# Gate rows stacked as two rounded parts, expert results turned half by half, two output biases moved from GpSimd to TensorE

## Time and profile before

| | us |
|---|---|
| median of 3 timed runs (lowest to highest) | 660.68 (659.87 to 660.93) |
| the profiled execution | 657.71 |
| its span, first to last instruction | 655.92 |
| TensorE busy in the span | 611.8 (93%) |
| VectorE busy | 484.3 (74%) |
| ScalarE busy | 358.9 (55%) |
| GpSimd busy | 201.1 (31%) |
| mean granted clock of TensorE, share of full speed | 0.949 |

### The profile page before, as it was taken

How to read it: one execution, slowest core, us unless ns; L and a number is a source line. 1 busy time by engine, 2 the same in 40 slices (tenths; PEclk the granted TensorE clock), 3 DMA queues, 4 the chain that set the end, 5 groups by cost and what they waited for, 6 DMA issues and landing times.

```text
span 655.9 us, 11543 instructions
## 1 busy us (share of the span) xinstructions
PE 611.8 (93%) x3408; PEld 441.0 (67%) x3408; DVE 484.3 (74%) x1247; ACT 358.9 (55%) x634; POOL 201.1 (31%) x454
## 2 busy tenths in 40 slices
PE   8999999898999879988999899999997999989996
PEld 5784788556676547855666548888775777744785
DVE  6666799968676468988653539999869888565796
ACT  6333455425666444535565228888734565623785
POOL 4211646540002113521120106666530000211462
PEclk9987999978999989999999769999997999997899
DMA  9225999010000017810002046777310000003571
GB/s 290 70 87 166 216 205 205 14 48 3 11 20 3 2 33 180 200 33 2 6 4 74 0 153 207 238 243 242 112 32 2 3 27 3 4 0 109 176 245 58
DMA packets 32526, 61.10 MB, mean 93 GB/s; under 512 B 6434, under 2 KB 21314, under 8 KB 32476
## 3 DMA queue, kind: packets, MB, share of 16 engines
q1 hardware_dynamic: 31900, 59.46, 31.6%
q10 hardware_dynamic: 576, 1.02, 0.5%
HBM read 55.64 MB, written 4.29 MB: 91 GB/s over the span
## 4 chain that ended last, share of the span: by engine, by line
PE 78%; DVE 11%; ACT 5%; issue 3%; DMA 1%; POOL 1%; DVEq 0%; SPq 0%; ACTq 0%
PE PS L744 12%; PE PS L745 12%; PE PS L746 12%; PE PS L1004 5%; PE PS L912 4%; PE PS L987 4%; PE PS L588 3%; PE PS L775 3%; PE PS L984 2%; PE PS L1021 2%; ACT pT L1307 2%; PE PS L960 1%; PE PS L809 1%; DVE qst L1660 1%; PE PS L941 1%
## 5 line engine op out<-in xcount | busy, mean ns | idle before, releaser
L479 POOL TENSOR_TENSOR wpair<-ring,ones_col 128x128 fp32r<-128x128 f32 (+1 forms) x150 | 66.7, 444 | 171.4 <-PE PS L746 104.8
L1307 ACT ACTIVATE pT<-PS 128x512 f32<-128x512 f32 x160 | 92.7, 595 | 45.8 <-PE PS L987 37.4
L1601 DVE TENSOR_TENSOR PS<-PS,qst 128x512 f32<-128x512 f32 x134 | 93.2, 696 | 20.7 <-ACT PS L1200 18.3
L1607 DVE TENSOR_TENSOR hid_lo<-PS,hid_hi 128x512 fp32r<-128x512 f32 x150 | 102.4, 683 | 1.7 <-ACT hid_hi L1206 1.3
L1206 ACT ACTIVATE hid_hi<-PS 128x512 fp32r<-128x512 f32 x150 | 89.2, 594 | 19.7 <-DVE PS L1601 19.4
L744 PE MATMUL PS<-xhi,wpair 128*128 128x512 f32 x204 | 85.5, 419 | 0.5 <-DVE PS L1589 0.4
L745 PE MATMUL PS<-xlo,wpair 128*128 128x512 f32 x204 | 83.4, 409 | 0.0
L746 PE MATMUL PS<-xhi,wpair 128*128 128x512 f32 x204 | 83.1, 407 | 0.0
L481 POOL TENSOR_TENSOR wpair<-ring,wpair 128x128 fp32r<-128x128 f32 (+1 forms) x150 | 76.8, 512 | 11.8
L1200 ACT ACTIVATE PS<-PS,ring 128x512 f32<-128x512 f32 x88 | 58.3, 662 | 30.3 <-PE PS L746 29.4
L987 PE MATMUL PS<-qst,kz 128*128 128x256 f32 x256 | 64.6, 337 | 2.9 <-ACT pT L1307 2.9
(11 more groups left out here) (236 smaller groups left out, 1101.3 us busy)
## 6 DMA issues: line engine op xcount, KB each, us to landing
qst<-gates SPq DMA_DIRECT2D x44, 512.0 KB, 4.9
qst<-gates SPq DMA_DIRECT2D x46, 256.0 KB, 5.7
ring<-in_mlp SPq DMA_DIRECT2D x48, 128.5 KB, 3.1
ring<-in_glu SPq DMA_DIRECT2D x27, 192.0 KB, 5.7
kz<-keys SPq DMA_DIRECT2D x36, 96.0 KB
keys<-qst SPq DMA_DIRECT2D x6, 512.0 KB, 3.6
qst<-kfull SPq DMA_DIRECT2D x96, 4.0 KB
wq<-in_wq SPq DMA_DIRECT2D x3, 256.0 KB, 3.5
```

Source lines behind the costliest of these rows:

```text
L479: pool.tensor_tensor(wpair[:, pair, 0, c], w, ones, ALU.mult).then_inc(M["wstep"], 1)
L1307: act.activation(pT[:, w % 8, :], PS[:, 2 + w % 2, :], ACT.Exp, scale=sc).then_inc(A["p"], 1)
L1601: dve.tensor_tensor(o, src, row, ALU.mult).then_inc(M["hid"], 1)
L1607: dve.tensor_tensor(hid_lo[:, kept, :], PS[:, gate_bank(glu, kept), :], hid_hi[:, kept, :].bitcast(f32), ALU.subtract).then_inc(M["lo"], 1)
```

## The change

- *Gate rows as a stack.* The turned table is rounded by ScalarE (both halves) into partitions 0 to 31 of `row_pair`, VectorE subtracts and writes the rest into partitions 32 to 63, both `f32r`. A spread is one rounded product over 64 rows with a matrix that picks the row twice. ScalarE then makes both plain copies `gate_rows`, which only the DRAM store needs. The rows go to banks 0 and 1 in layers 0 and 1. `row_pair` lies where the split query weights were, so the keys of layer 2 move to `hid_hi`/`hid_lo`.
- *Start of the result banks.* In layers 2 and 3 the zero products are gone; the biases are split in setup (four small VectorE operations, and one for the picking matrix) and added by two rounded products per half. In layer 2 the unit-matrix products go ahead of the fillers.
- *Order at the route.* The table is turned before the up-projections of units 2 and 3, not behind them; fillers there are 6 and 6 in layers 2 and 3 (8 and 4 before).
- *Turn by halves.* `turn_back(L, 0)` stands before the last down-projection, `turn_back(L, 1)` behind it; ScalarE copies both halves. Fillers behind it: 8 in layers 0 and 1, none in layer 2 (16 each before).
- *Masked counts of layer 3.* Two before the turning of the normalised tile, one behind it, one behind the first query projections; fillers there 2, not 6.
- *Output biases.* `output_bias` and the transfers of `bo` are gone. The bias lies with the other bias rows, and `project_outputs` starts its bank with one product of ones and bias, before it waits for its operand.
- *SyncE.* In layer 1 the keys of layer 2 are saved ahead of the gates. The output is stored in two halves.

```diff
+        row_pair = wqpair[0:2 * EP, :, :]
+        rows_hi, rows_lo = row_pair[0:EP, :, :], row_pair[EP:2 * EP, :, :]
...
@@ SyncE, load_ring
+                if L == 1:
+                    save_keys(2)
                 save_gates()
                 first_gates()
                 if L == 1:
-                    save_keys(2)
                     stack_keys(2, range(1))
...
@@ TensorE
+            def turn_back(L, hf):
+
+                pe.wait_ge(y_out, NHALF * L + hf + 1)
+                for k in range(4):
+                    i = 4 * hf + k
+                    mm = pe.transpose(PS[:, 2 + hf, k * P:(k + 1) * P], yT[:, i * P:(i + 1) * P], ident)
+                mm.then_inc(y_turned, 1)
...
                     if first:
                         pe.wait_ge(M["hid"], kept % 2 + 1)
+                        pe.wait_ge(rt["lo"], NHALF * L + hf + 1)
...
-                        w = consts[0:EP, C_ID3 + entry:C_ID3 + entry + 1].broadcast_to([EP, P])
-                    pe.matmul(PS[:, gate_bank(glu, kept), :], w, gate_rows[:, hf, :], start=True, stop=True).then_inc(M["spread"], 1)
+                        if first and unit >= 2:
+                            pe.wait_ge(rows_out, NHALF * L + hf + 1)
+                        w = pick_one[:, entry:entry + 1].broadcast_to([2 * EP, P])
+                    pe.matmul(PS[:, gate_bank(glu, kept), :], w, row_pair[:, hf, :], start=True, stop=True).then_inc(M["spread"], 1)
...
-                keep_busy(0, (0, 2, 8, 4)[L])
+                if L == 2:
+                    pe.wait_ge(set_dve, 3)
+                    for hf in range(NHALF):
+                        c = slice(hf * HALF, (hf + 1) * HALF)
+                        pe.matmul(PS[:, hf, :], eye[:, :], xhi[:, c], start=True, stop=False, skip_group_check=True)
+                        pe.matmul(PS[:, hf, :], eye[:, :], xlo[:, c], start=False, stop=False, skip_group_check=True)
+                keep_busy(5 if L == 2 else 4 if L == 3 else 0, (0, 2, 6, 6)[L])
+                turn_rows(L)
                 if not glu:
                     for u in (2, 3):
                         up(u, 1, 1, u % 2)
-                turn_rows(L)
-                pe.wait_ge(rows_out, NHALF * (L + 1))
...
+                    if glu:
+                        pe.wait_ge(rows_out, NHALF * L + hf + 1)
+                        mm = pe.matmul(PS[:, hf, :], zerob[:, 0:P], zerob[:, :], start=True, stop=False, skip_group_check=True)
+                    else:
+                        for part in range(2):
+                            mm = pe.matmul(PS[:, hf, :], b2pair[L][:, part, :], row_pair[:, hf, :], start=(L == 3 and part == 0),
+                                           stop=False, skip_group_check=True)
...
-                if L < 3:
-                    keep_busy(4, 16)
+                turn_back(L, 1)
+                if L < 2:
+                    keep_busy(4, 8)
...
@@ project_outputs
-                    pe.wait_ge(A["fin_e"], pre["fin_e"] + hf + 1)
                     if hf == 1:
                         pe.wait_ge(A["p"], pre["p"] + adds_of[L]["p"])
+                    if L != 2:
+                        r = 2 * WIDE + 2 * P + (L // 2) * P
+                        pe.matmul(PS[:, 1 + hf, :], ones2[:, 0:P], brow[:, r:r + P].unsqueeze(1).broadcast_to([P, 4, P]),
+                                  start=True, stop=False, skip_group_check=True)
+                    pe.wait_ge(A["fin_e"], pre["fin_e"] + hf + 1)
...
@@ ScalarE, experts
-                act.wait_ge(rt["tr"], NHALF * (L + 1))
-                act.activation(gate_rows[:, 1, :], PS[0:EP, 7, :], ACT.Copy).then_inc(rows_out, 1)
+                for hf in range(NHALF):
+                    act.wait_ge(rt["tr"], NHALF * L + hf + 1)
+                    act.activation(rows_hi[:, hf, :], PS[0:EP, row_bank(L, hf), :], ACT.Copy).then_inc(rt["hi"], 1)
+                for hf in range(NHALF):
+                    act.wait_ge(rt["lo"], NHALF * L + hf + 1)
+                    act.activation(gate_rows[:, hf, :], PS[0:EP, row_bank(L, hf), :], ACT.Copy).then_inc(rows_out, 1)
```

More of the change, by code:

```diff
@@ L56 @@
 WIDE = HGRP * P
-BROWS = 2 * WIDE + 2 * P
+BROWS = 2 * WIDE + 4 * P
 C_ALL = C_BAND + TB * S
@@ L1205, in first_part @@
                         act.wait_ge(M["y"], u + 1 + UP_AHEAD - KEPT)
+                    elif L == 1 and u == 2:
+                        act.wait_ge(k_saved[2], 48)
                     act.activation(hid_hi[:, kept, :], PS[:, gate_bank(glu, kept), :], ACT.Copy).then_inc(M["hi"], 1)
-                early = 2 if glu else KEPT
-                for u in range(early):
+                for u in range(2):
                     unit(u, u // 2, u % KEPT, first=True)
@@ L1215, in experts @@
                         key_low(half)
[L1216 to L1217 removed]
+                for hf in range(NHALF):
+                    act.wait_ge(rt["tr"], NHALF * L + hf + 1)
+                    act.activation(rows_hi[:, hf, :], PS[0:EP, row_bank(L, hf), :], ACT.Copy).then_inc(rt["hi"], 1)
+                for hf in range(NHALF):
+                    act.wait_ge(rt["lo"], NHALF * L + hf + 1)
+                    act.activation(gate_rows[:, hf, :], PS[0:EP, row_bank(L, hf), :], ACT.Copy).then_inc(rows_out, 1)
                 for u in range(2 * RING):
[L1219 to L1220 removed]
+                    if u >= 2:
+                        unit(u, u // 2, u % KEPT, first=(u < KEPT))
                     if u > 0:
@@ L1266, in take_outputs @@
                     act.activation(o, banks(4), ACT.Copy).then_inc(A["oe"], 1)
+                if L == 3:
+                    for b in range(2):
+                        take_masked(b)
                 layer_norm(2 * L, (0,))
+                if L == 3:
+                    take_masked(2)
                 for a in range(HGRP):
+                    if L == 3 and a == HGRP - 1:
+                        take_masked(3)
                     take_queries(0, a, 2 + a)
@@ L1771, in constants @@
     c[:, C_IOTA:C_IOTA + HD] = np.arange(HD)
-    c[:EP, C_ID3:C_ID3 + EP] = np.eye(EP)
+    c[:2 * EP, C_ID3:C_ID3 + EP] = np.tile(np.eye(EP), (2, 1))
     row = np.arange(P) % 32 // HD
```

146 lines of the change are left out of this document (69 added, 77 removed).

## The result

The changed kernel takes 635.86 us (635.11 to 637.94), the kernel before 660.63 beside it: a ratio of 0.9632, 95% interval 0.9608 to 0.9656. The forecast was 638.1. The profiled execution of the changed kernel took 636.07, its span 634.28; before they were 657.71 and 655.92. So the spans differ by 21.6 us, the medians by 24.8. The difference lies in which executions were profiled: that of before was 2.9 us under its own median, that of after 0.2 above.

What follows compares the result with a forecast made beforehand. TensorE was taken to bound the kernel (busy 93% of the span, 78% of the chain). Terms summed to 23.6 us, less one for the clock 22.6: 635.1 for the profiled execution, 638.1 for the median; range 629 to 647.

Steps and rivals of the forecast that it cites:

- Route of layer 2: Gate table to first experts, layer 2: next up-projection at 380.3, not 389.63; gain 8.8 us after 1.5 stall, bounds 7 and 10.3.
- rival of plain products: All routes: rounded spread is not one pass, 24 spread and bias products stay at 0.9 us; 15.6 back, 653.7; chance 0.03.
- Route of layer 3: Gate table to first experts, layer 3: 7.7 us with the first pair, less the same stall; gain 6.3, bounds 4.5 and 7.7.
- Route of layer 0: Gate table to first experts, layer 0: worth 5 us by TensorE alone, but loads hold it; gain 1.2, bounds 0 and 5.
- The rival by which layer 0 is not held by its loads: Layer 0: its loads do not hold it, so 3.8 us more are gained, 634.3; chance 0.15.
- Route of layer 1: Gate table to first experts, layer 1: cheaper later spreads, ring refill about 3 us forward; gain 1.6 us, bounds 0.5 and 2.2.
- The clock, one microsecond in reserve: Any turn or route: one microsecond taken off for meeting the half clock where it did not before.
- the rival of the falling clock: Starts of stages after turns and routes: TensorE at half clock with fewer fillers; 8.3 us given back, 646.4; chance 0.15.
- Turn behind layer 0: Layer 0 results to next LayerNorm: earlier first half, fillers 16 to 8 ending at 139.0; gain 1.9 us, bounds 0.5 and 3.4.
- Turn behind layer 2: Layer 2 results to next LayerNorm: earlier turn 0.85 us, masked counts spread over waits; gain 3.2, bounds 2 and 4.
- The end: End of kernel: last down-projection waits 0.7 us for first copy, store halved; loss 0.3, bounds gain 0.3 and loss 0.7.
- loads that hold layers 2 and 3: Rival, layers 2 and 3: gates and ring slots arrive as late as before, halving both routes' gain; +7.5 us, 645.6; chance 0.12.

Runs made afterwards that it cites:

- e7: Changed kernel with plain fp32 spreads and bias products over 32 rows instead of rounded ones over 64; 659.37 us, ratio 0.9989.
- e1: Changed kernel with the 16 spreads and 8 bias products as plain fp32 over the same 64 rows; 643.98 us, ratio 0.9724.
- e2: Changed kernel with plain fp32 spreads in layer 0 alone (four products); 637.94 us, ratio 0.9650.
- e5: Changed kernel with three groups of layer 0 loads not yet needed (masks, value windows, stacked keys) put later in SyncE's list; 632.38 us, ratio 0.9561.
- e10: Changed kernel with e5's late loads, both halves turned behind the last down-projection in layers 2 and 3, and eleven more fillers; 630.48 us, ratio 0.9537.
- e11: Changed kernel with layer 3's masked counts in one block ahead of turning the normalised tile, as before; 635.62 us, ratio 0.9621.
- e12: Changed kernel with the 16 fillers of before behind the turn of layer 2, counts still spread; 638.04 us, ratio 0.9681.
- e3: Changed kernel with both halves turned behind the last down-projection in all layers; 634.94 us, ratio 0.9606.
- e4: Changed kernel without the eight fillers behind the turns of layers 0 and 1; 638.33 us, ratio 0.9658.

## Why the prediction was right, and where it was not

The sum of 22.6 us stands against 21.6 in the spans, and the big terms held in place and, within 0.7 us, in size: both large routes, the turn behind layer 1, the end. By step:

- **Route of layer 2, 8.8 forecast, 8.76 measured.** First up near the place given (380.3 forecast; 375.18 plus the 4.61 by which the layer was ahead is 379.8), stall 1.4 for 1.5. The reason given for the clock was half right: e7 shows that plain products over 32 rows lower it there, e1 that plain products over 64 rows do not. By these traces the row stack is worth more by what goes with its rows, the clock above all (e7 less e1: 3.6 and 5.2 us in layers 2 and 3), than by the price of the product (2.6 and 2.9). The prediction's rival of plain products put 15.6 us on the form of all 24; e1 took 8, and 1.8 of them by the clock behind layer 0.
- **Route of layer 3, 6.3, measured 5.62.** The same mechanism and the same kind of stall (VectorE waits 1.76 us for gate rows at 589.31). Both parts were set too high: 6.5 us are won by the first down-projection, where 7.7 were forecast, and 0.9 is given back, where 1.5 was.
- **Route of layer 0, 1.2, measured 0.70.** 4.86 us were won at the first down-projection and all but 0.7 given back on the ring loads; e2 and e5 show it from both sides. The size is not sharp: the seven traces with this layer 0 differ among themselves by 2 us and would give 0.7 to 2.7, with 1.2 among them. The rival by which layer 0 is not held by its loads is refuted for this order of SyncE, and made true by e5.
- **Route of layer 1, 1.6, measured 0.57.** 1.43 us are won by the first down-projection and 0.86 given back in the loop, which the term had at nothing: GpSimd waits 4.20 us for the first refill of the ring, and TensorE 0.59 behind it. The refill is issued 5.1 us earlier than before (248.65 and 253.73), 3 of them by the new order as forecast, and it is late even so.

```profile
253.59 0.61 POOL L486 TENSOR_TENSOR wpair<-ring,ones_col 128x256 fp32r<-128x256 f32 x1 [4.20 <-DMA ring<-in_glu]
...
255.06 0.50 PE L745 MATMUL PS<-xhi,wpair 128*128 128x512 f32 x1 [0.59 <-POOL wpair L488]
```

- **The clock, one microsecond in reserve.** 1.20 us are lost at the router of layer 1, where the half stretch moved onto the wait and the router, so the rival of the falling clock happened here in small. Attention 1 lost 0.50 beside its biases and attention 3 gained 0.15. Their cause is open: the traces with the same attention 1 differ by a microsecond there. Together, with 0.05 in attention 2, it is -1.6 and not -1.0.
- **Turn behind layer 0, 1.9, measured 3.75.** The forecast took the half clock of before as given (eight fillers at half clock ending at 139.0). It ran at 1.00; e1, where it fell again, has the projection 1.8 us later. That is the error of this term, nearly all of it. The clock stayed at 1.00 there in nine of the twelve traces with eight fillers, and fell in e1, e2 and e10.
- **Turn behind layer 2, 3.2, measured 2.87 to the first scores, by another step than given.** I had put 2.35 on spreading the counts and nothing on the 16 fillers in front of them. By e11 the spreading is worth 0.3, by e12 the fillers 2.7. The error was to price the block and not to ask what it stood behind.
- **The end, -0.3, measured -0.14:** two effects that nearly cancel, 1.4 lost by the halves (e3), 1.3 gained by splitting copies, waits and store. Which of the three gave the 1.3 was not tried.
- **Biases, -0.8, measured -0.47; setup, -0.3, measured -0.37.** Traces with the same setup differ by up to 0.9 us at this point (53.62 in e12, 54.48 in e1), so the match of setup is luck.
- **The other rivals.** A spread that is not one pass is refuted by the four products in 1.41 us; loads that hold layers 2 and 3 cost 1.4 and 0.9 us where the sum had 1.5 each, not half of the gain; no expert loop stayed at half clock. Neither sign of being wrong came: the first up-projection of layer 2 waits for ScalarE (0.32), not for gate rows or ring, and the clock behind the three turns is at 1.00.

The sum was better than its terms by luck, since errors of opposite sign cancel. The turn behind layer 0 gave 1.85 us more than forecast, and the biases cost 0.3 less. The routes of layers 1, 3 and 0 gave 1.0, 0.7 and 0.5 less, the turn behind layer 2 gave 0.3 less, and the clock took 0.6 more. And the timed medians moved by 2.2 us more than the sum, since the profiled execution of before was a fast one; that the offset carries over as a difference was an assumption that failed.

## What to carry to other kernels

When a stage that loads a lot gets a faster start, look at what is queued in front of its next refill: the gain of 4.5 us was there, and only taking loads that nobody needed yet out of the way kept most of it. Before pricing a block of work that is moved, look at what holds its start. And short plain products over few rows cost twice here, once by themselves and once by the clock that the following work got: try stacking operands to more rows where that is free. A last one: compare several traces of the same stage before you explain a microsecond. Here one stage with the same code differed by 2 us between executions, and a half clock came and went behind layer 0 with edits that left that stage as it was.

## What the runs showed of the hardware that was not expected

- Plain fp32 products over 32 rows, with TensorE recorded busy in every microsecond, were followed by a granted clock of 0.50 (6.8 us in layer 2, 10.2 in layer 3, e7). The same number over 64 rows, in the same places and at the same 0.9 us each, kept 1.00 (e1). That is one trace of each; the mean clock of the timed runs, 0.938 to 0.955 and 0.960 to 0.973, goes the same way.
- Half-clock stretches move and change their length when a few microseconds of work are shifted or filled (router of layer 1: 234.6 to 238.0 before, 228.1 to 234.9 after, 229.6 to 233.0 in e3, 228.2 to 238.4 in e4, 234.6 to 238.0 in e10).
- The DMA engines were at a share of 1.04 with 212 GB/s in layer 0 of e5, and at 0.90 with 313 GB/s in layer 2 of the kernel after; gate rows are broadcast in both. The share says that they are full or nearly so, the bytes do not.
